# Decoder layer with routed experts: VectorE steps of the gating stage moved to other engines, second expert's weights and seven output tiles requested later

## The reference

```
x = x + attn(layernorm(x), ...)          # four layers of width 128, then back to 1024
# second step: for every batch and channel the 154 largest of 256 entries of ctx are the "crucial" ones
x1 = layernorm(x)
crucial, sub = mask * x1, (1 - mask) * x1
A1, A2 = sigmoid(relu(batchnorm(conv(max and mean of crucial)))), the same of sub
x = x + crucial * A1 + sub * A2
# third step: eight experts of 1024 x 1024, two per token
x2 = layernorm(x)
top_vals, top_idx = top_k(x2 @ gate_w, 2);  p = softmax(top_vals)
x = x + sum over the two chosen experts of p * (x2 @ expert_w[e])
```

## Time and profile before

| | |
|---|---|
| median of three runs | 1124.79 us (1124.30 to 1128.26) |
| the profiled execution | 1125.29 us, span 1123.5 us |
| PE busy | 1009.7 us, 90% of the span |
| DVE, ACT, POOL busy | 565.4, 373.1, 446.7 us |
| PE clock, mean over the span | 0.951 of full speed |
| DMA | 120.25 MB, 107 GB/s over the span |

### The profile page before, as it was taken

One profiled execution on the slowest core, in us unless ns is written; L12 is line 12 of the kernel. 1 busy time (PEld: TensorE's weight loads), 2 busy tenths in 40 slices (PEclk: granted clock), 3 DMA queues, 4 the chain that ended last, 5 costly groups with the idle time before them and its releaser, 6 DMA issues. The chain is left out here.

```text
span 1123.5 us, 13340 instructions
## 1 busy us (share of the span) xinstructions
PE 1009.7 (90%) x3528; PEld 533.5 (47%) x3535; DVE 565.4 (50%) x1661; ACT 373.1 (33%) x1014; POOL 446.7 (40%) x562
## 2 busy tenths in 40 slices
PE   6788889999998969799737999999999999999995
PEld 6686555555544435334423444444444444444442
DVE  5645789999986879969985111111111111111111
ACT  2433768778764338668620000000000000000000
POOL 3833456455552010009505444444344443333331
PEclk9878999999998989999868999999999999999998
DMA  7320111110000330004695373464637346373332
GB/s 301 132 75 1 48 48 39 57 39 1 1 1 1 150 132 20 1 1 169 259 381 184 75 223 76 110 192 123 183 79 230 81 131 174 77 224 75 75 75 38
DMA packets 38462, 120.25 MB, mean 107 GB/s; under 512 B 6220, under 2 KB 9351, under 8 KB 38408
## 3 DMA queue, kind: packets, MB, share of 16 engines
q1 hardware_dynamic: 25592, 79.77, 19.3%
q0 software_dynamic: 12816, 39.86, 16.3%
HBM read 82.91 MB, written 36.70 MB: 106 GB/s over the span
## 5 line engine op out<-in xcount | busy, mean ns | idle before, releaser
L2008 PE MATMUL bank<-T,X 128*128 x1184 | 508.4, 592 | 0.8 <-DVE X L2056 0.8
L2008 PEld LDWEIGHTS bank<-T,X 128*128 128x128 f32 x1184 | 224.9, 190 | 284.0 <-issue 284.0
L2070 DVE TENSOR_SCALAR X<-bank,col_p 128x512 f32<-128x512 f32 x37 | 27.8, 751 | 399.5 <-PE bank L2008 399.5
L2036 ACT ACTIVATE X<-bank,col_p 128x512 f32<-128x512 f32 x37 | 25.4, 687 | 495.1 <-PE bank L2008 495.1
L1961 POOL DMA_INDIRECT X<-x_nrm,col_s x156 | 150.6, 965 | 71.6 <-issue 46.9
L1970 POOL DMA_INDIRECT out_dram<-X,col_d x37 | 60.0, 1621 | 262.8 <-DVE X L2070 244.3
L470 POOL TENSOR_TENSOR rs<-ve,neg_half 128x4 f32<-128x4 f32 x36 | 37.4, 1040 | 116.8 <-DVE ve L951 116.8
L636 PE MATMUL bank<-nat,T 128*128 128x512 f32 x128 | 69.9, 677 | 10.5 <-issue 7.8
L817 ACT ACTIVATE M<-X,T 128x256 bf16<-128x256 f32 x152 | 74.9, 496 | 0.5 <-POOLq L466 0.5
L805 ACT ACTIVATE X<-bank,T 128x512 f32<-128x512 f32 x64 | 43.9, 687 | 58.3 <-PE bank L636 56.7
L226 POOL TENSOR_TENSOR late<-late,neg_half 128x1 f32<-128x1 f32 x32 | 17.8, 556 | 112.6 <-DVE late L222 112.6
(11 more groups left out here) (333 smaller groups left out, 1444.1 us busy)
## 6 DMA issues: line engine op xcount, KB each, us to landing
T<-in_L_ffn_expert_w_dram SPq DMA_DIRECT2D x8, 4096.0 KB, 17.5
out_dram<-X SPq DMA_DIRECT2D x17, 512.0 KB
M<-in_x_dram SPq DMA_DIRECT2D x16, 512.0 KB, 7.3
X<-in_x_dram SPq DMA_DIRECT2D x16, 512.0 KB, 6.3
x_nrm<-H SPq DMA_DIRECT2D x16, 512.0 KB, 3.5
T<-in_ctx_dram SPq DMA_DIRECT2D x9, 512.0 KB, 3.6
X<-x_nrm,col_s POOLq DMA_INDIRECT x156, 3.6
X<-in_ctx_dram SPq DMA_DIRECT2D x4, 512.0 KB, 7.0
```

What stands on the lines that cost most here:

```text
L2008: mm = nc.tensor.matmul(bank[2 * u + n][:, :], xgt[u][:, k, :], Tf[:, ds(odd * D + (k * N + n * BANK), BANK)], start=(k == 0), stop=(k == ...
```

## The change

- In batch 0 DVE makes the first half of the factors itself (four TENSOR_SCALAR, L1866 of the new file) while ACT makes the second half; the count of `gmul` is one lower throughout. The sum of gate_w (`g_part`) stands ahead of the sigmoid's result.
- `back_shift` is a TENSOR_SCALAR with two scalar operands per partition, in place of a SCALAR_TENSOR_TENSOR.
- The two steps `shift` and `known + shift` behind batch 2 run on POOL, behind its powers of batch 2 and ahead of its products of batch 5.
- In batches 5, 6 and 7 the first tile's statistics leave DVE: the additions of `residual` also give the sums (TENSOR_TENSOR_REDUCE), DVE makes the mean of them (one small step), ACT squares the deviations with a running sum (`squared`, 128x1024), POOL scales the sum and raises it to the power.
- `second_sums` stands ahead of `stats` in every batch, and in batch 7 between the two tiles of `stats`. The last `shift` and `known` steps stand ahead of the wait for the last transposed logits.
- ACT's constants for the routing (`sel`, `lane_row`, `tile_base`) stand ahead of the last four `normed` instead of ahead of the last two.
- SP stores only the tiles 0 to 8 of X within the loop; the other seven are stored behind the last row of x_nrm, with a semaphore `out_late` for which the first addition to `out` waits. The gathers wait for nine tiles and not for sixteen.
- Expert 1's weights are requested in the next block, once two slots of rows are transposed.

PE's instructions and their order are the same. The diff, cut to these:

```diff
+        FIRST_SQUARED = B - 3
+
+        def on_scalar(b, h):
+            return b >= FIRST_SQUARED and h == 0
+
+        def counted(m, t):
+
+            return m * NT + t + 1 - (sum(on_scalar(*divmod(i, CT)) for i in range(t + 1)) if m == 1 else 0)
...
+        KEPT_TILES = 3 * IN_FLIGHT
...
-            wait(gmul, 2 * b + n + 1)
+            if 2 * b + n > 0:
+                wait(gmul, 2 * b + n)
...
@@ -1464,8 +1478,9 @@
                 for b in range(B):
                     for h in range(CT):
                         t = b * CT + h
-                        sp.wait_ge(x2_done, 4 * b + 2 + h + 1)
-                        sp.dma_start(out[t * P:(t + 1) * P, :], X[:, t, :]).then_inc(out_init, 16)
+                        if t < KEPT_TILES:
+                            sp.wait_ge(x2_done, 4 * b + 2 + h + 1)
+                            sp.dma_start(out[t * P:(t + 1) * P, :], X[:, t, :]).then_inc(out_init, 16)
                         sp.wait_ge(ln_out, NT + t + 1)
                         sp.dma_start(x_nrm[1 + t * P:1 + (t + 1) * P, :], nring[h]).then_inc(nrm_st[h], 16)
                     if b == B // 2:
@@ -1473,11 +1488,11 @@
                         sp.wait_ge(p1_mm, P1 + B // 2)
                         sp.dma_start(wslot[:, 0, :, :], expert_src(0)).then_inc(w_in_sem[0], 16)
 
+                sp.dma_start(x_nrm[0:1, :], nring[0][0:1, :]).then_inc(out_init, 16)
                 sp.dma_start(out[N:N + P, :], X[:, 0, :]).then_inc(out_init, 16)
-                sp.dma_start(x_nrm[0:1, :], nring[0][0:1, :]).then_inc(out_init, 16)
-                sp.wait_ge(back_mm, 4 * B)
-                sp.wait_ge(p1_mm, P1 + B)
-                sp.dma_start(wslot[:, 1, :, :], expert_src(1)).then_inc(w_in_sem[1], 16)
+                for t in range(KEPT_TILES, NT):
+                    sp.wait_ge(x2_done, 4 * (t // CT) + 2 + t % CT + 1)
+                    sp.dma_start(out[t * P:(t + 1) * P, :], X[:, t, :]).then_inc(out_late, 16)
...
+                        if on_scalar(b, h):
+                            t = b * CT + h
+                            pool.wait_ge(g_act, G_SQUARES + t // CT - FIRST_SQUARED + 1)
+                            nc.gpsimd.tensor_scalar(ve_all(1)[:, t:t + 1], ve_all(1)[:, t:t + 1], 1.0 / D, EPS, ALU.mult, ALU.add).then_inc(g_pool, 1)
+                            pool.wait_ge(g_pool, G_KNOWN + t // CT - FIRST_SQUARED + 1)
                         ln_pow(pool, 1, b * CT + h)
+                    if b == 2:
+                        pool.wait_ge(l_set, 3)
+                        nc.gpsimd.tensor_tensor(shift, mean_all(0).unsqueeze(2).to_broadcast([P, NT, E]), g_all.unsqueeze(1).to_broadcast([P, NT, E]), ALU.mult).then_inc(g_pool, 1)
+                        pool.wait_ge(g_pool, G_KNOWN - 1)
+                        nc.gpsimd.tensor_tensor(known, known, shift, ALU.add).then_inc(g_pool, 1)
...
-                        hold(act, g_dve, 11)
-                    for k in range(KD):
+                        hold(act, g_dve, 12)
+                    for k in range(KU if b == 0 else 0, KD):
...
+                def squared(b):
+                    t = CT * b
+                    hold(act, g_dve, G_GATES + b - FIRST_SQUARED + 1)
+                    a.activation(M[:, 0:KU, b * S:(b + 1) * S], X[:, t, :].rearrange("p (k s) -> p k s", k=KU), ACT.Square,
+                                 scale=-1.0, bias=mean_of(1, t), accum_out=ve_all(1)[:, t:t + 1]).then_inc(g_act, 1)
...
+                    if b >= FIRST_SQUARED:
+                        squared(b)
+                    if b == B - 1:
+                        hold(act, g_act, G_SQUARES + B - FIRST_SQUARED)
+                        for k in range(QK):
+                            a.copy(sel[:, k, :].rearrange("p (i b) -> p i b", i=QK), ident[:, k * QP:(k + 1) * QP].unsqueeze(1).to_broadcast([P, QK, QP])).then_inc(r_sel, 1)
+                        a.copy(lane_row, iota_lane[:, :]).then_inc(r_sel, 1)
+                        a.activation(tile_base, step_t[:, 0, :].unsqueeze(2).to_broadcast([P, NT, WIDE]), ACT.Copy, scale=float(QK)).then_inc(r_sel, 1)
...
-                            v.tensor_tensor(part, part, bank[BACK[2 * h + n]][:, :], ALU.add).then_inc(x2_done, 1)
+                            if on_scalar(b, h):
+                                v.tensor_tensor_reduce(part, part, bank[BACK[2 * h + n]][:, :], 1.0, 0.0, ALU.add, ALU.add, half_sum[b % 2][:, n:n + 1]).then_inc(x2_done, 1)
+                            else:
+                                v.tensor_tensor(part, part, bank[BACK[2 * h + n]][:, :], ALU.add).then_inc(x2_done, 1)
...
                         hold(dve, x2_done, 4 * b + 3 + h)
-                        ln_stats(dve, 1, CT * b + h)
+                        if on_scalar(b, h):
+                            v.tensor_scalar(mean_of(1, CT * b), half_sum[b % 2][:, 0:1], half_sum[b % 2][:, 1:2], 1.0 / D, ALU.add, ALU.mult).then_inc(g_dve, 1)
+                        else:
+                            if b == B - 1:
+                                second_sums(b)
+                            ln_stats(dve, 1, CT * b + h)
...
-                    v.scalar_tensor_tensor(back_of(1, t), mean_of(1, t), -1.0, rstd_of(1, t), ALU.mult, ALU.mult).then_inc(ln_nb, 1)
+                    v.tensor_scalar(back_of(1, t), mean_of(1, t), rstd_of(1, t), -1.0, ALU.mult, ALU.mult).then_inc(ln_nb, 1)
...
+                for k in range(KU):
+                    ins = v.tensor_scalar(gsel[0][:, k, :], M[:, k, 0:S], z[:, 0, k * B:k * B + 1], z[:, 1, k * B:k * B + 1], ALU.mult, ALU.add)
+                ins.then_inc(g_dve, 1)
+                hold(dve, g_dve, G_GATES)
...
                         behind(b - 1)
+                        second_sums(b - 1)
                     stats(b)
-                    if b > 0:
-                        second_sums(b - 1)
...
-                        then(v.tensor_tensor(shift, over_e(mean_all(0)), over_t(g_all), ALU.mult))
-                        then(v.tensor_tensor(known, known, shift, ALU.add))
...
-                second_sums(B - 1)
+                hold(dve, ln_mean, counted(1, NT - 1))
+                hold(dve, g_dve, G_GATES + B - FIRST_SQUARED)
+                hold(dve, g_pool, G_KNOWN)
+                then(v.tensor_tensor(shift, over_e(mean_all(1)), over_t(g_all), ALU.mult))
+                then(v.tensor_tensor(known, known, shift, ALU.subtract))
                 dve.wait_ge(l_mm, B)
                 then(v.tensor_tensor(known, known, bank[P2_BANK][:, 0:NT * E].rearrange("p (t e) -> p t e", e=E), ALU.add))
-                then(v.tensor_tensor(shift, over_e(mean_all(1)), over_t(g_all), ALU.mult))
-                then(v.tensor_tensor(known, known, shift, ALU.subtract))
                 behind(B - 1)
...
-                for w in range(2):
-                    sp.wait_ge(w_in_sem[w], 16)
-                    sp.sem_inc(w_ready, 1)
+                sp.wait_ge(w_in_sem[0], 16)
+                sp.sem_inc(w_ready, 1)
+                sp.wait_ge(xg_tp, 2)
+                sp.dma_start(wslot[:, 1, :, :], expert_src(1)).then_inc(w_in_sem[1], 16)
+                sp.wait_ge(w_in_sem[1], 16)
+                sp.sem_inc(w_ready, 1)
...
-                pool.wait_ge(out_init, NT * 16 + 32)
+                pool.wait_ge(out_init, KEPT_TILES * 16 + 32)
...
+                    if u == 0:
+                        pool.wait_ge(out_late, (NT - KEPT_TILES) * 16)
```

More of the change, by code:

```diff
@@ L193, in decoder_kernel @@
         JUNK = D + BANK + P // 2
-        assert JUNK + S <= 2 * D - 10 * NT
+        assert JUNK + S + 4 <= 2 * D - 10 * NT
         def mean_of(m, t):
@@ L212, in back_of @@
             return norm_at[m][:, 4 * NT + t:4 * NT + t + 1]
+        FIRST_SQUARED = B - 3
[3 more added lines that the diff above has]
+            return m * NT + t + 1 - (sum(on_scalar(*divmod(i, CT)) for i in range(t + 1)) if m == 1 else 0)
         def ln_stats(dve, m, t):
             v = nc.vector
-            u, n = t % TPC, m * NT + t + 1
+            u, n = t % TPC, counted(m, t)
             v.bn_stats(st6[:, u, 0:6], X[:, t, 0:BANK])
@@ L224, in ln_pow @@
         def ln_pow(pool, m, t):
-            pool.wait_ge(ln_var, m * NT + t + 1)
+            pool.wait_ge(ln_var, counted(m, t))
             nc.gpsimd.tensor_tensor(rstd_of(m, t), ve_all(m)[:, t:t + 1], neg_half[:, 0:1], ALU.pow).then_inc(ln_rstd, 1)
@@ L1432, in decoder_kernel @@
         wslot = T[:, :, :].rearrange("p k (w n) -> p w k n", w=2)
-        out_init = sem("out_init")
+        out_init, out_late = sem("out_init"), sem("out_late")
+        KEPT_TILES = 3 * IN_FLIGHT
         w_in_sem = [sem(f"w_in{w}") for w in range(2)]
@@ L1443, in expert_src @@
             return expert_w[e, :, :].rearrange("(k p) n -> p k n", p=P)
+        half_sum = [late[:, JUNK + S + 2 * u:JUNK + S + 2 * u + 2] for u in range(2)]
+        G_GATES, G_KNOWN, G_SQUARES = 13, 3, 1
         def gated_half(eng, b, n, wait):
-            wait(gmul, 2 * b + n + 1)
+            if 2 * b + n > 0:
+                wait(gmul, 2 * b + n)
```

(6 more changed lines are left out.)

## The result

| | before | after |
|---|---|---|
| median (runs) | 1124.95 us (4) | 1113.98 us (4; 1112.39 to 1115.86) |
| profiled execution, span | 1125.29, 1123.5 | 1115.55, 1113.7 |
| PE's loop starts, lasts | 601.95, 508.41 | 592.19, 508.41 |
| DVE's last step of the block | 590.67 | 577.30 |
| next block opens for DVE | 591.79 | 582.09 |

The ratio is 0.9896, with a 95% interval of 0.9882 to 0.991: 1.0% faster. Two later sets of runs of the same kernel gave 0.9902 [0.9887, 0.9917] and 0.9904 [0.9888, 0.992].

The account below looks back on a forecast made before the run. PE's expert loop (508.41 us) keeps its length, so only its start moves, mostly by DVE's gating. Gains 1.5 + 0.7 + 4.83 + 2.8 + 1.3 = 11.1, taken as 10.8: 1114.5 profiled, 1114.0 median, range 1112 to 1118.5.

Parts of the forecast that it names:

- front, batch 0: Start of gating: DVE and ACT share the factors, so batch 0's additions start 1.5 us earlier (1.0 to 2.2).
- to batch 2: Batches 1 and 2: the TENSOR_SCALAR shift saves 2.2 us, but DVE then waits for PE; 0.7 more gained.
- behind batch 2: Ahead of batch 3's additions: all 4.83 us of the two moved steps and their stretch goes from DVE.
- batches 3 to 7: Batches 5 and 6: statistics leaving DVE save 1.4 us each, 2.8 in all; DVE's batch falls to 5.3.
- batch 7 to the logits: Last batch: 1.4 us less statistics, 0.5 of PE wait covered, 0.6 lost at the moved copy; net 1.3.
- logits to the block: Same instructions, 21.2 us, no gain counted; SP ends near 578.5, just in time for the block at 580.1.
- block to the loop: From the next block's opening to PE's expert loop: same instructions, 10.2 us, no gain counted.
- PE's margin: Gating batches: PE needs 6.0 us a batch but enters batch 5 over 2 us ahead, so DVE still sets batch 7.
- rival 1: SP late at the block's end, last store issued after DVE's last step: costs 1 to 5, taken 2.5, 1116.5 us; chance 0.15.
- seven stores of about 0.5 more: End of SP's queue in the gating block: each late store's issue adds about 0.5 us, ending near 578.5.
- Rivals 2 to 4: DVE stalls beside POOL (1117, 0.09); ACT's squared(7) waits for a store (1123, 0.06); PE runs dry in loop (1129, 0.02).
- the page that spoke against the change: DVE and GpSimd share an exclusive port lock, so the new TENSOR_SCALARs might still stall; tied to the second rival, 0.09.

Follow-up runs that it names:

- e1: The changed kernel again, nothing edited: four runs, 1114.32 to 1115.37 us.
- e11: The changed kernel, unedited, run as partner of e12 on the same chip: 1115.36 us (1114.09 to 1116.51).
- e9: Kernel before, with only DVE making the first half of batch 0's factors: 1126.56 us, ratio 1.0006.
- e5: Kernel before, with only the shift -mean * rstd made a TENSOR_SCALAR: 1125.09 us, ratio 0.9994.
- e6: Kernel before, with only the two steps shift and known + shift behind batch 2 on POOL: 1121.28 us, ratio 0.9958.
- e8: e7 with all statistics back on DVE, no squares on ACT: 1117.40 us, ratio 0.9921.
- e2: Changed kernel, with the seven late stores moved to the head of SP's queue in the next block: 1116.55 us, ratio 0.9909.
- e7: Changed kernel, with the seven late stores in the next block behind the first transposed slot: 1113.36 us, ratio 0.989.
- e12: The version of e7 once more, beside the unedited changed kernel on one chip: 1110.62 us, ratio 0.9856.
- e3: Changed kernel with SP's old queue (all sixteen tiles stored as they come, expert 1's weights requested at the gating block's end): 1120.56 us, ratio 0.9952.
- e4: Kernel before, with only SP's queue changed to the new one: 1124.79 us, ratio 0.9989.

## Why the prediction was right, and where it was not

1114.0 was forecast and 1113.98 measured, and that it is so close is luck. Two terms were 2.0 too small together and a wait of 3.5 that stood among the rivals came true. That left the profiled execution at 1115.55 where 1114.5 was forecast for it, and the median of four lies between two executions at 1112.4 and two at 1115.7; over all 13 executions of this kernel (first four, e1, e11) it is 1115.21. By its own steps, in gains behind the common start:

| step | forecast | measured |
|---|---|---|
| front, batch 0 | 1.5 | 1.60 |
| to batch 2 | 0.7 | 0.51 |
| behind batch 2 | 4.83 | 4.74 |
| batches 3 to 7 | 2.8 | 3.97 |
| batch 7 to the logits | 1.3 | 2.14 |
| logits to the block | 0 | -3.51 |
| block to the loop | 0 | 0.06 |

- **Front.** The size was right, but what stood behind it was not said. e9 shows that alone it is worth nothing (the loop starts 0.6 later): it moves DVE's shift into two of POOL's products. It needs the TENSOR_SCALAR shift: at batch 2 e9 alone loses 0.35, e5 alone gains 0.50, and the changed kernel, which has both, gains 2.11 (the two without the rest were not run).
- **Batches 1 and 2.** DVE waited 1.53 us at the copy (1.3 forecast) and batch 2 came at 520.09 (520.1). That only a part can be had is e5's 0.86.
- **Behind batch 2.** Right. e6 alone brings 4.68 at this station.
- **Batches 3 to 7.** The term that was mis-sized. I put 0.08 more on an addition that sums; it costs nothing, since the read of the sum is hidden. Batches 5 and 6 take 4.93 and not 5.3. The other 0.7 are stand-stills of the old shift beside POOL at batches 4 and 5 (0.57 and 0.58 us for a pair, in place of 0.22), which the trace of before showed and I had not counted. By e8 the squares bring 5.0 in all.
- **Batch 7 to the logits.** 0.8 more than forecast: I let the moved copy wait 0.6 for PE. It did not wait, by 0.25 us (553.59 against 549.72 + 3.62).
- **PE's margin.** I had 6.0 us a batch for PE, and it is 5.66. PE now runs without a printed wait from 503.50 to 553.34, so little more is to be had from DVE in this stage. PE by time, changed kernel:

```profile
541.94 1.97 PE L1586 MATMUL bank<-ident,T 128*128 128x128 f32 x16
...
547.60 1.97 PE L1586 MATMUL bank<-ident,T 128*128 128x128 f32 x16
549.50 0.29 PE L1612 MATMUL bank<-ident,fin 8*128 8x8 f32 x2
549.72 3.62 PE L1605 MATMUL bank<-T,gate 128*8 128x256 f32 x16
```

- **Behind the logits.** Here the forecast failed, and rival 1 came true at 3.5 where I priced it 2.5. Its sign came too: SP issued its last store at 580.3, and DVE's last step had begun at 577.30. The failed step is "seven stores of about 0.5 more". Seven issues took 8.03, their median 1.19: 0.5 is what a store's issue took where others were not waiting ahead of it, and the seven need no others to wait for, since in e2 they took 6.98 from idle DMA engines on. In the changed kernel 512 KB in 1.19 us is 440 GB/s (the engines moved 402 over 575 to 580 us), so an issue behind a full queue seems to take as long as a store ahead of it moves; the earlier trace rows had a 1.13 behind two others and I didn't use it. e7 and e12 show the whole price: 3.5 to 3.6. With the logits 2 earlier than forecast DVE also had more to wait.
- **What the queue's change was for.** I gave the rows' early landing a gain in no term, and took SP's end as the one thing it moves. e3 shows what it buys, 5.4: the exponential on ACT and the first gather would be late without it. e4 shows that it moves no station as long as DVE is late itself.
- **Rivals 2 to 4.** No small DVE step beside POOL was above 0.33 us; `squared(7)` waited 1.43 for DVE and for no store; the loop had no gap, and expert 1's weights, requested at 597.03, landed 16.8 later.
- **What stays open:** why two of the first four runs were 3 us shorter. Profiles of one kernel (changed, e1 and e11) differ ahead of the gating by up to 0.9 us and those of e7 and e12 by 2.2, and hardly behind it, and this goes with the clock granted there (see e1); but none was of such a run, and what sets that clock from one execution to the next is not shown. Not tried alone were the places of `second_sums` and of ACT's constants.

On the page that spoke against the change: the Trainium skill, "SBUF — State Buffer", section "SBUF: two separate sides", has DVE and GpSimd exclude each other for a whole instruction where DVE reads two SBUF inputs. The runs agree for SCALAR_TENSOR_TENSOR and TENSOR_TENSOR on `late` (2.44 us for the shift's pair beside one product, 4.39 beside two; 2.30 and 2.31 for the 128x128 steps). The one-column TENSOR_SCALAR with two scalar operands went free (0.32 beside a product), and so did the additions with one input from a bank. The four TENSOR_SCALAR of 128x256 ended before POOL's first product began at 503.61, so no run shows what they would do beside one.

## What to carry to other kernels

An edit's worth depends on what stands next to it: half the factors on DVE were worth nothing until the step they ran into had another form, and the new DMA order nothing until DVE was fast enough to need it. So count each edit with and without the others. When work is moved to the end of a queue that a barrier waits for, price its issues as the queue will be there, full, and look for a place behind the barrier and behind the first transfer that the next stage needs. Compare profiles from an instruction behind which the kernels differ, not from the start of the span.
